# Filler matmuls on TensorE ahead of its waits in the gather passes of a four-layer graph network

## The chip, the cores and the metric

The kernel runs on one core of one Trainium2 chip. The metric is the device time of one execution in microseconds. Before the change it is 6958.88 us, the median of three runs (6939.15 to 6967.73).

## The reference

Four graph layers run one after the other over 6250 nodes of 128 features and 100,000 edges, sorted by their target. Each layer's result is added to its input and layer-normalised:

```python
edge_index = jnp.stack([src, dst])
x = _layernorm(x + L0(edge_index, x))              # attention of one head
x = _layernorm(x + L1(x, edge_index, edge_attr_3)) # attention of four heads
x = _layernorm(x + L2(x, edge_index))              # edge MLP
x = _layernorm(x + L3(x, edge_index, edge_weight)) # two graph convolutions
```

Every layer takes rows of a node table by an edge's index, weights them per edge, and sums them into the edge's other node (`segment_sum`): in L0 and L1 `h[src]` with softmax weights into `dst`, in L2 two SiLU products of both nodes' features into `row`, in L3 twice `h[row] * norm` into `col`.

## The kernel before

Between the gather passes stand short node passes, which do the dense products, the layer norm and write the table for the next pass to HBM. The gather passes take nearly all of the time. There are five of them, by four pieces of code: L0 (first pass, unrolled), L1 (second, a loop of four steps per turn), L2 (third, a loop of twelve groups per turn) and `convolution`, which is called twice.

In all of them GpSimd fetches edge tiles: one indirect DMA takes 128 rows of the table by 128 indices in `idx_now` into a ring in SBUF. L0 and L1 have 208 steps of four such gathers (`gather`, L664); L2 (L1852) and each convolution (L2246) have 784 gathers in groups of eight and 104 groups of steps. VectorE builds one-hot matrices of the target within a tile of 128 nodes (L934, L1998, L2313: tensor_scalar), TensorE multiplies them with the rows, which sums them by node (L1069, L1406, L1953, L2296), and VectorE adds the product from PSUM to `acc` (L965, L1436 and L1442, L2008, L2323). ScalarE weights the rows (`wide`) and copies the indices of later steps into `idx_now`, which lets GpSimd go on.

The order of each engine's work is the program's order; semaphores tie the engines to each other. On TensorE the steps are these:

- L0 `step`: wait for `l0_wide` (ScalarE) and `l0_acc` (VectorE), then four products (L1069), and in some steps eight transposes for a sort that VectorE runs beside the pass. `spread_last` multiplies once into banks 6 and 7, which VectorE reads as `pair[3]`.
- L1 `step`: the sum of the step two back (L1406), the queries of the next step (L1397), then wait for `l1_gm` and one product (L1417) that spreads the step's maximum; VectorE waits for it at L1489 in the same step.
- L2 `step`: `own_half` of the group two ahead (L1922, 24 products), `turn` of the next (L1932), `second_product` of this (L1937, L1941), `summed` of the one before (L1948, L1953).
- `convolution` `step`: wait for a cleared window, two zero products (L2290), wait for the one-hots and for the landed tiles (`rows_of` reads from a table how many are needed), eight sums (L2296), two closing products (L2299).

VectorE in L2 makes the transposed one-hots of a later group (L1981) as soon as TensorE has used up the older ones. After the sum of a convolution group it adds (L2323), clears the window (L2326) and makes the one-hots of the next group (L2313).

An fp32 product shows in the trace as two matmuls with a weight load each. PSUM has eight banks of 512 words per partition; `pair[n]` is banks 2n and 2n + 1.

## Time and profile before

| | us |
|---|---|
| median of the runs | 6958.88 |
| lowest and highest | 6939.15, 6967.73 |
| profiled execution, first to last instruction | 5685.5 |
| median less that span | 1273.4 |
| GpSimd busy | 3958.0 |
| VectorE busy | 3263.6 |
| TensorE busy | 3113.8 |
| ScalarE busy | 1491.5 |

The profile gives the span of its execution, and no time for the execution as a whole, so what the runs hold beside the span can only be had as a difference to their median. The page prints each engine's busy share in 40 slices and below them the clock that TensorE was granted (PEclk, in tenths of 2.4 GHz; 5 is 1.2 GHz). Matmuls overlap each other, so a mean duration times a count is more than the busy time. GpSimd's time in a gather is the making of the transfer, not the transfer.

### The profile page before, as it was taken

How to read it: one execution, taken by the hardware profiler on the slowest of the kernel's cores; microseconds unless marked ns; L12 is line 12 of the kernel's file. 1: busy time of each engine (PE TensorE's matmuls, PEld its weight loads, DVE VectorE, ACT ScalarE, POOL GpSimd, SP SyncE). 2: the span in 40 equal slices, each digit the busy share in tenths (PEclk: the TensorE clock that was granted, in tenths of full speed). 3: DMA queues.
4: the chain of work that ended last, by engine and by line, in shares of the span. 5: the costliest groups of instructions: out<-in, count | busy, mean ns of one | idle time of the engine just before them, and what ended most of it. 6: DMA issues, size and time to landing. Idle time of an engine off the chain costs nothing. (4 is left out here: it accounts for less than half of the span.)

```text
span 5685.5 us, 82572 instructions
## 1 busy us (share of the span) xinstructions
PE 3113.8 (55%) x17051; PEld 2734.5 (48%) x17052; DVE 3263.6 (57%) x12090; ACT 1491.5 (26%) x5626; POOL 3958.0 (70%) x4054
## 2 busy tenths in 40 slices
PE   4444444356666666778898988433333443333333
PEld 3333333345555555657777776333333343333332
DVE  6888887676787787744444444433444443344445
ACT  2333333345555555532222223100000000000001
POOL 3777777736777777367777772677777757777774
PEclk7555555568888777865555556666666666666666
DMA  5111112214444444222121110111111121111112
GB/s 123 52 52 52 52 52 56 49 52 131 132 132 131 130 131 131 70 54 56 52 56 51 53 52 21 56 52 51 51 51 51 51 61 52 51 51 51 51 51 57
DMA packets 222234, 385.68 MB, mean 68 GB/s; under 512 B 85452, under 2 KB 121882, under 8 KB 221998
## 3 DMA queue, kind: packets, MB, share of 16 engines
q0 software_dynamic: 142944, 296.35, 19.0%
q1 hardware_dynamic: 79054, 86.72, 5.0%
q8 instruction: 83, 1.36, 0.1%
q14 instruction: 153, 1.25, 0.1%
HBM read 356.23 MB, written 26.56 MB: 67 GB/s over the span
## 5 line engine op out<-in xcount | busy, mean ns | idle before, releaser
L2246 POOL DMA_INDIRECT arena<-table_gcn,idx_now x1568 | 1532.2, 977 | 642.9 <-issue 422.1
L2296 PE MATMUL pair<-arena,hotf 128*128 x3328 | 726.6, 408 | 1224.7 <-POOLq L1819 1199.3
L2296 PEld LDWEIGHTS pair<-arena,hotf 128*128 128x128 f32 x3328 | 691.2, 317 | 1256.1 <-issue 1255.8
L664 POOL DMA_INDIRECT arena<-table_attention,idx_now x832 | 825.7, 992 | 272.7 <-issue 197.2
L664 POOL DMA_INDIRECT arena<-table_key_value,idx_now x832 | 789.2, 949 | 275.9 <-issue 221.1
L1852 POOL DMA_INDIRECT arena<-table_edge_mlp,idx_now x784 | 768.1, 980 | 261.2 <-issue 212.4
L2323 DVE TENSOR_TENSOR acc<-acc,pair 128x1024 f32 x208 | 253.9, 1221 | 1133.9 <-PE pair L2299 1133.9
L1069 PE MATMUL pair<-wide,hotf 128*128 128x130 f32 x1664 | 431.0, 439 | 653.3 <-ACT wide L1033 653.3
L1069 PEld LDWEIGHTS pair<-wide,hotf 128*128 128x128 f32 x1664 | 369.0, 326 | 718.5 <-ACT wide L1033 718.5
L2256 ACT COPY idx_now<-src_t 128x8 int32 (+1 forms) x204 | 39.3, 197 | 1815.2 <-PE pair L2299 1803.2
L1406 PE MATMUL pair<-wide,hotf 128*128 128x132 f32 x1664 | 314.1, 347 | 232.9 <-DVE acc L1436 232.8
L1991 DVE TENSOR_TENSOR hot<-pair,arena 128x64 f32<-128x64 f32 x832 | 132.8, 224 | 492.1 <-POOLq L1819 456.7
L2313 DVE TENSOR_SCALAR hotf<-iota,rel_now,ew_now 128x128 f32<-128x128 f32 x1664 | 406.5, 331 | 0.0
L1406 PEld LDWEIGHTS pair<-wide,hotf 128*128 128x128 f32 x1664 | 267.6, 241 | 272.9 <-issue 270.5
L1953 PE MATMUL pair<-wide,hotf 128*128 128x64 f32 x1664 | 373.8, 418 | 0.0
L1953 PEld LDWEIGHTS pair<-wide,hotf 128*128 128x128 f32 x1664 | 354.6, 324 | 6.5
L1397 PE MATMUL pair<-arena 128*128 x1664 | 307.6, 347 | 8.5 <-DVE arena L1453 8.5
L1397 PEld LDWEIGHTS pair<-arena 128*128 128x128 f32 x1664 | 293.2, 264 | 9.1 <-issue 8.9
L1349 ACT ACTIVATE junk<-iota,rel_now 128x128 f32<-128x128 f32 x832 | 265.7, 390 | 18.3 <-ACT idx_now L652 12.9
L1033 ACT ACTIVATE wide<-arena,small 128x129 f32<-128x129 f32 x832 | 267.0, 393 | 0.0
L1468 DVE TENSOR_TENSOR junk<-pair,arena 128x512 f32<-128x512 f32 x208 | 143.9, 692 | 204.4 <-DMA arena<-table_key_value,idx_now 204.2
L938 DVE SCALAR_TENSOR_TENSOR junk<-iota,rel_now,arena 128x128 f32<-128x128 f32 x832 | 256.4, 344 | 0.0
(371 smaller groups left out, 5709.7 us busy)
## 6 DMA issues: line engine op xcount, KB each, us to landing
key<-rel_dram SPq DMA_DIRECT2D x104, 256.0 KB, 3.4
arena<-rel_dram SPq DMA_DIRECT2D x52, 512.0 KB, 3.7
arena<-table_gcn,idx_now POOLq DMA_INDIRECT x1568, 2.5
arena<-table_attention,idx_now POOLq DMA_INDIRECT x832
arena<-table_key_value,idx_now POOLq DMA_INDIRECT x832
arena<-table_edge_mlp,idx_now POOLq DMA_INDIRECT x784, 2.4
table_attention<-arena SPq DMA_DIRECT2D x13, 512.0 KB, 3.0
table_gcn<-acc SPq DMA_DIRECT2D x26, 256.0 KB, 2.3
```

What stands on the lines that cost most here:

```text
L664: q_.indirect_dma_start(ring[:, slot, 0:width], None, table, bass.IndirectOffsetOnAxis(ap=idx_now[:, slot:slot + 1].bitcast(U32), axis=0)) ...
L938: last = v.scalar_tensor_tensor(out=junk[:, 0, u * P:(u + 1) * P], in0=iota[:, :], scalar=rel_now[:, g * G + u:g * G + u + 1], in1=dst_sco ...
L1033: last = s_.activation(wide[:, g, u, 0:D + 1], ring[:, g * G + u, 0:D + 1], ACT.Identity, scale=small[:, g, u:u + 1])
L1069: last = t_.matmul(bank[2 * (g % 2) + u // 2][:, (u % 2) * AW:(u % 2) * AW + D + 2], hotf[:, g, u, :], wide[:, g, u, 0:D + 2], start=True, ...
L1349: last = s_.activation(away[:, u * P:(u + 1) * P], iota[:, :], ACT.Abs, scale=-1.0, bias=rel_now[:, g * G + u:g * G + u + 1])
L1397: last = t_.matmul(QB[g % 2][:, u * P:(u + 1) * P], hotT_f[:, g, u * P:(u + 1) * P], flat(look[:, bass.ds(nodes[u], 1), :]), start=True, s ...
L1406: last = t_.matmul(bank[SUM + 2 * (g % 2) + u // 2][:, (u % 2) * AW:(u % 2 + 1) * AW], hotf[:, g, u, :], wide[:, g, u, :], start=True, sto ...
L1852: q_.indirect_dma_start(mlp_ring[:, slot * EH:(slot + 1) * EH], None, t2, bass.IndirectOffsetOnAxis(ap=idx_now[:, slot:slot + 1].bitcast(U ...
L1953: last = t_.matmul(window[:, bass.ds(offset * EH, EH)], hot8[:, g % 2, u, :], s2[:, g % 2, u * EH:(u + 1) * EH], start=False, stop=(u == C ...
L2246: q_.indirect_dma_start(conv_ring[:, slot * D:(slot + 1) * D], None, table, bass.IndirectOffsetOnAxis(ap=idx_now[:, slot:slot + 1].bitcast ...
L2296: t_.matmul(window[:, bass.ds(offset * D, D)], hot8[:, g % 2, u, :], conv_ring[:, bass.ds(slot * D, D)], start=False, stop=False)
L2313: last = v.tensor_scalar(out=hot8[:, g % 2, u, :], in0=iota[:, :], scalar1=rel_now[:, at], scalar2=ew_now[:, at], op0=ALU.is_equal, op1=AL ...
```

## The change

A helper `keep_busy(spare, times)` issues matmuls of a constant bf16 identity with a constant bf16 row of numbers, repeated four times to 512 columns, into a PSUM bank. Nothing reads that bank's content. It is called on TensorE once per step in all gather passes: 12 times before the wait for `wide` in L0 (bank 7), 6 times before the wait for the maximum in L1 (bank 0), 10 times between `second_product` and `summed` in L2 (bank 3), and 24 times before the wait for the cleared window in the convolutions (bank 7). To leave bank 7 free in L0, `spread_last` goes to banks 4 and 5 and VectorE reads `pair[2]`. `rows_of` now loads its register and takes the maximum with 0 into a second one.

```diff
--- before.py
+++ after.py
@@ -688,6 +688,11 @@
                 batch(b, 2, 2)
             batch(NB - 2, 2, 1)
             batch(NB - 1, 2, 0)
+
+        def keep_busy(spare, times):
+
+            for _ in range(times):
+                t_.matmul(spare, ident_b[:, :], iota_b[:, :].unsqueeze(1).to_broadcast([P, 4, P]), start=True, stop=True)
 
         NORM = BT + 1
 
@@ -865,7 +870,7 @@
                     dve.wait_ge(sort_lastB, 1)
                     ch(v.scalar_tensor_tensor(out=key[:, :].rearrange("q (b p) -> q b p", **by_block),
                                               in0=iota[:, :].unsqueeze(1).to_broadcast([P, SORT // P, P]), scalar=float(SORT // P),
-                                              in1=pair[3][:, :].rearrange("q (b p) -> q b p", **by_block), op0=ALU.mult, op1=ALU.add))
+                                              in1=pair[2][:, :].rearrange("q (b p) -> q b p", **by_block), op0=ALU.mult, op1=ALU.add))
                     counts, e, node, base = (tiny[:, n, :] for n in range(4))
                     for b in range(SB):
                         yield
@@ -1058,11 +1063,12 @@
                     pe.wait_ge(pick_made, 1)
                     pe.wait_ge(sort_last, 1)
                     for h in range(2):
-                        last = t_.matmul(bank[6 + h], pick_last[:, :], last_tile[:, h * 512:(h + 1) * 512], start=True, stop=True)
+                        last = t_.matmul(bank[4 + h], pick_last[:, :], last_tile[:, h * 512:(h + 1) * 512], start=True, stop=True)
                     last.then_inc(sort_lastB, 1)
 
                 def step(i, g, past, left):
                     k = i * RING + g
+                    keep_busy(bank[7], 12)
                     pe.wait_ge(l0_wide, k + 1)
                     pe.wait_ge(l0_acc[G - 1], k + 1)
                     for u in range(G):
@@ -1413,6 +1419,7 @@
                         summed(*later(i, g, -2))
                     if left:
                         query(*later(i, g, 1))
+                    keep_busy(bank[0], 6)
                     pe.wait_ge(l1_gm, k + 1)
                     t_.matmul(MB[:, 0:P], small[:, g, 0:1].to_broadcast([P, P]), ident[:, :], start=True, stop=True).then_inc(l1_gmB, 1)
 
@@ -1822,8 +1829,10 @@
 
         def rows_of(eng, need, table, k):
 
-            eng.reg_load([need], table[0:1, bass.ds(k, 1)])
-            return eng.snap(need, min_val=0, max_val=CTILE_GROUPS - 1) + 1
+            loaded, bounded = need
+            eng.reg_load([loaded], table[0:1, bass.ds(k, 1)])
+            eng.reg_alu(bounded, loaded, 0, ALU.max)
+            return eng.snap(bounded, min_val=0, max_val=CTILE_GROUPS - 1) + 1
 
         def at_least(eng, signal, k, more):
 
@@ -1960,6 +1969,7 @@
                     if not isinstance(k, int) or k + 1 < CSTEP_GROUPS:
                         turn(k + 1, g + 1)
                     second_product(k, g)
+                    keep_busy(bank[3], 10)
                     if not isinstance(k, int) or k > 0:
                         summed(k - 1, g - 1 + CRING)
 
@@ -1973,7 +1983,7 @@
             def _(dve):
                 first = [dve.alloc_register(f"l2_node{g}") for g in range(2)]
                 slots = [dve.alloc_register(f"l2_slot{u}") for u in range(CG)]
-                need = dve.alloc_register("l2_need")
+                need = [dve.alloc_register(f"l2_need{n}") for n in range(2)]
 
                 def hot_look(i, g, k):
                     dve.wait_ge(l2_rel_in[g % 4 // 2], 16 * (k // 4 + 1) if isinstance(k, int) else 4 * k - 4 * (g % 4) + 16)
@@ -2279,12 +2289,13 @@
                 def _(pe):
                     slots = [pe.alloc_register(f"{name}_slot{u}") for u in range(CG)]
                     offsets = [pe.alloc_register(f"{name}_offset{u}") for u in range(CG)]
-                    need = pe.alloc_register(f"{name}_need")
+                    need = [pe.alloc_register(f"{name}_need{n}") for n in range(2)]
 
                     def step(i, g, k):
                         window = pair[g % 3]
                         pe.reg_load(slots, step_slot[0:1, bass.ds(k * CG, CG)])
                         pe.reg_load(offsets, step_offset[0:1, bass.ds(k * CG, CG)])
+                        keep_busy(bank[7], 24)
                         pe.wait_ge(cleared, k + 1)
                         for h in range(2):
                             t_.matmul(window[:, h * 512:h * 512 + D], zeros[:, 0:P], zeros[:, 0:D], start=True, stop=False)
```

## Rows read from the trace of the kernel before

**Rows 1.** The page, 40 slices: GpSimd's busy tenths, TensorE's granted clock in tenths.

```profile
POOL 3777777736777777367777772677777757777774
PEclk7555555568888777865555556666666666666666
```

**Rows 2.** Windows, four passes: stretch, PE, PEld, DVE, ACT, POOL busy, clock, DMA, GB/s.

```profile
102.60:1199.50 1096.90, 457.23 (x1785) 392.86 (x1786) 846.21 (x4115) 409.29 (x1884) 832.30 (x839) 0.51 0.21 52
1305.50:2347.80 1042.30, 677.45 (x3719) 608.14 (x3719) 822.74 (x2883) 559.43 (x2073) 789.17 (x832) 0.80 0.44 131
2450.90:3457.70 1006.80, 872.08 (x5516) 752.37 (x5517) 440.10 (x1936) 201.62 (x501) 768.11 (x784) 0.52 0.19 53
3583.80:4588.30 1004.50, 389.04 (x2060) 359.76 (x2060) 419.73 (x1050) 39.81 (x296) 765.88 (x784) 0.67 0.18 51
```

**Rows 3.** Timeline: start us, us, engine, line, operation, idle time before.

```profile
4016.84 0.94 POOL L2246 DMA_INDIRECT arena<-table_gcn,idx_now  x1 [0.30 <-issue]
...
3421.25 1.47 POOL L1852 DMA_INDIRECT arena<-table_edge_mlp,idx_now  x1 [0.30 <-DMA arena<-table_edge_mlp,idx_now]
3421.49 0.42 DVE L1981 TENSOR_SCALAR hotT<-arena,part 128x1024 bf16<-128x1024 bf16 x1
```

**Rows 4.** Grouped lines, GpSimd's gathers: busy us, mean ns | idle before.

```profile
L2246 POOL DMA_INDIRECT arena<-table_gcn,idx_now x1568 | 1532.2, 977 | 642.9 <-issue 422.1 <-ACT ew_now L2261 165.6 <-DMA arena<-table_gcn,idx_now 55.2
L664 POOL DMA_INDIRECT arena<-table_attention,idx_now x832 | 825.7, 992 | 272.7 <-issue 197.2 <-DMA arena<-table_attention,idx_now 42.7 <-ACT idx_now L652 32.8
L664 POOL DMA_INDIRECT arena<-table_key_value,idx_now x832 | 789.2, 949 | 275.9 <-issue 221.1 <-DMA arena<-table_key_value,idx_now 31.7 <-ACT idx_now L652 23.1
L1852 POOL DMA_INDIRECT arena<-table_edge_mlp,idx_now x784 | 768.1, 980 | 261.2 <-issue 212.4 <-DMA arena<-table_edge_mlp,idx_now 26.2 <-ACT rel_now L1878 22.6
```

**Rows 5.** Waits: engine, line, releaser: us in total, times, longest.

```profile
PE pair L2296 <- POOLq L1819: 1199.3, 192, 12.2
...
DVE junk L1468 <- DMA arena<-table_key_value,idx_now: 204.2, 206, 4.1
```

**Rows 6.** Timeline, third pass: 24 matmuls of 64 columns, one of 512, bf16.

```profile
2943.98 1.49 PE L1922 MATMUL pair<-arena,hotT 128*128 x24
...
2947.45 0.60 PE L1937 MATMUL pair<-tab 3*128 3x512 bf16 x1
```

**Rows 7.** Timeline, second pass: L1417 at 1.2 GHz, then a step at 2.4.

```profile
1705.20 0.80 PE L1417 MATMUL pair<-ident,small 128*128 128x128 f32 x2
...
1707.01 1.14 PE L1406 MATMUL pair<-wide,hotf 128*128 128x132 f32 x8 [1.01 <-DVE acc L1436]
...
1707.98 1.05 PE L1397 MATMUL pair<-arena 128*128 x8
...
1710.28 0.49 PE L1417 MATMUL pair<-ident,small 128*128 128x128 f32 x2 [1.24 <-DVE small L1480]
```

**Rows 8.** Timeline, convolutions: a group's matmuls at either clock.

```profile
4006.73 3.55 PE L2296 MATMUL pair<-arena,hotf 128*128 x16 [2.42 <-POOLq L1819]
...
5628.43 2.23 PE L2296 MATMUL pair<-arena,hotf 128*128 x16
...
5636.12 3.49 PEld L2296 LDWEIGHTS pair<-arena,hotf 128*128 128x128 f32 x16 [4.51 <-issue]
```

**Rows 9.** Windows of 1 us: a convolution group, then the third pass.

```profile
4006.00:4007.00 1.00, 0.27 (x1) 0.30 (x2) 1.00 (x3) 0.00 (x0) 0.70 (x2) 0.76 0.21 57
...
4010.00:4011.00 1.00, 0.55 (x7) 0.25 (x5) 0.44 (x1) 0.39 (x3) 0.70 (x2) 1.00 0.02 4
...
2943.00:2944.00 1.00, 1.00 (x7) 1.00 (x7) 0.00 (x0) 0.00 (x0) 0.94 (x1) 0.50 0.16 33
```

**Rows 10.** Timeline, ends of the third and the first pass.

```profile
3464.26 1.06 PE L1932 MATMUL pair<-ident,junk 128*128 128x128 f32 x4
...
3481.85 0.69 DVE L2008 TENSOR_TENSOR acc<-acc,pair 128x512 f32 x1 [3.08 <-PE pair L1953]
...
1204.18 2.10 PE L1069 MATMUL pair<-wide,hotf 128*128 128x130 f32 x8 [3.86 <-ACT wide L1033]
```

## Prediction

> **What bounds the kernel now.** I read the page first. GpSimd's busy tenths stand at 7 in nearly every slice except at the ends of stages; TensorE's granted clock changes from slice to slice while GpSimd's share does not [rows 1]. So I cut the span into its gather passes, one stretch each [rows 2]; of the two convolutions, which are alike, one stands. They hold 1096.9 + 1042.3 + 1006.8 + 2 x 1004.5 = 5155 us of the span of 5685.5, and in each GpSimd is busy for 76% although TensorE's busy time runs from 389 to 872 us and its clock from 0.51 to 0.80. The rest of GpSimd's time is a fixed gap: the timeline shows a gather of 0.94 us with 0.30 us of "issue" before it, over and over, 1.25 us a gather with rounding [rows 3]. The grouped lines give 832 + 832 + 784 + 1568 = 4016 gathers [rows 4]. 4016 x 1.25 = 5020 us, and the means above 0.94 us account for most of what is left: 832 x 0.05 + 832 x 0.01 + 784 x 0.04 + 1568 x 0.035 = 136 us. That is 5156, the length of the passes. The kernel is paced by GpSimd issuing gathers back to back, and the waits of TensorE (1199 us for landed groups in the convolutions) are those of a faster engine for that pace [rows 5]. The longest wait of VectorE in the second pass, 204 us for gathered rows in 206 steps, says the same: about 1.0 us of slack in each step of 5.0 us [rows 5].
>
> **What TensorE would have to do.** The change puts filler matmuls on TensorE, which is in order: the wait behind the filler, and everything behind that wait, comes after it. The executed filler is 208 x 12 = 2496 matmuls in the first pass, 208 x 6 = 1248 in the second, 104 x 10 = 1040 in the third and 208 x 24 = 4992 in the two convolutions. A filler matmul streams 512 bf16 columns over one weight load. The trace has no such stream. The nearest is 24 bf16 matmuls of 64 columns in 1.49 us at the low clock, 62 ns or 0.97 ns a column, so 512 columns cost some 0.43 us at 1.2 GHz (columns over clock) and 0.21 us at 2.4 GHz (an estimate from that row and the two clock levels). The upper end is a lone 512-column bf16 matmul at 0.60 us [rows 6]. Now the budget of one step:
> - First pass: period 5.0 us (4 gathers); own matmuls 2.10 us at 1.2 GHz [rows 10], so half of it at 2.4; filler 12 x 0.43 = 5.1 or 12 x 0.21 = 2.6. Sum 7.2 or 3.6 us.
> - Second pass: period 5.0; own 1.14 + 1.05 + 0.49 less overlap = 2.5 at the high clock [rows 7]. The pass's busy time is 677/1042 of 5.0 = 3.25 at a mean clock of 0.80, that is 60% high and 40% low, so 0.6 x 2.5 + 0.4 x 4.4, and 4.4 at the low clock. Filler 2.6 or 1.3. Sum 7.0 or 3.8.
> - Third pass: period 10.0 (8 gathers); own 872/1007 of 10.0 = 8.7 at a mean clock of 0.52, or about 4.5; filler 4.3 or 2.1. Sum 13.0 or 6.6 [rows 2].
> - Convolutions: period 10.0; own 3.55 + 0.3 = 3.8 (high clock 2.23 + 0.3 = 2.5); filler 10.2 or 5.1. Sum 14.0 or 7.6 [rows 8].
>
> So at 2.4 GHz all four fit under the gathers and at 1.2 GHz none does. The whole change hangs on the granted clock. A mean clock of 0.5 x 13.0/10 = 0.65 is enough in the third pass, and 0.70 to 0.72 by the same working in the others.
>
> **Will the clock rise?** In a convolution the clock fell in the microsecond from 4006 (0.76), after TensorE had waited 2.42 us. Then a burst of 128-column matmuls began at 4006.73 and took 3.55 us, and in the microsecond from 4010 the clock was 1.00 again [rows 8, 9]. In the second pass, where TensorE works 65% of the time, the mean is 0.80. Against this stands the third pass: TensorE busy for 1.00 of a microsecond again and again and the clock still 0.50 [rows 9]. Much of that pass's work (L1922, L1953) loads 128 columns of weights to stream 64, so the array itself is fed half of the time. The filler streams 512 columns per load and is denser than what raised the clock in the convolutions, 24 and 12 of them in a row. And the mechanism corrects itself: a TensorE that falls behind at 1.2 GHz has no idle time at all, only dense filler and its own work. I take the clock to be near 1.0 in the first pass and the convolutions, 0.9 in the second, 0.7 to 0.9 in the third, where only a third of the time is filler and TensorE has the largest own load. The Trainium skill, TensorE: Matmul & The Clock Gate, Part 1, says that activity releases the throttle and idleness brings it back; the third pass shows that busy time as the profile counts it is not yet that activity.
>
> **What a faster TensorE is worth.** In the passes nothing directly: every microsecond that it gains it waits longer for GpSimd. Three things remain.
>
> Drains, the work after the last gather of a pass. Third pass: the last gather ends at 3457.7, VectorE's last add starts at 3481.85, and TensorE is the chain: turn, product, sum, product, sum, sum. From the turn at 3464.26 that is 17.5 us; at 2.4 GHz 8.8 + 2 fillers x 2.1 = 13.0, so -5 us (at 1.2 GHz 17.5 + 2 x 4.3, so +9) [rows 10]. First pass: the last four products, 2.10 us, halve: -1. Second pass: two such groups on the path: -2. Convolutions: the last three sums start some 3.8 us apart, at 5628.43 and, after a wait for the last tiles, at 5636.12. With 2.2 + 5.1 us before each of the last two, the last starts near 5624.6 + 2 x 7.5 = 5639.6, 3.5 us later than now, and takes 1.3 us less: +2 each [rows 8, 10]. Sum -1 - 2 - 5 + 2 + 2 = -4.
>
> Stretched gathers. Some gathers take up to 1.47 us instead of 0.94, when a VectorE tensor_scalar starts inside the first part of a gather: L1981 at 3421.49 in that from 3421.25 [rows 3]. L2313 does the same in the convolutions. The same instructions starting in the gap or late in a gather cost nothing. By the means against a plain gather's 0.944 us the excess is 0.036 x 784 = 28 us in the third pass and 0.033 x 1568 = 52 us in the convolutions [rows 4]. The start of these instructions follows TensorE: in the third pass L1981 comes after TensorE's `own_half`, which now queues behind 8.7 us of work a group; in the convolutions L2313 follows the sum by the add and the memset. With a faster TensorE the third pass's L1981 comes straight after the memset, another phase, and I book half of the 28 us: -14. In the convolutions the sum shortens from 3.5 to 2.2 us, 1.3 us, nearly one gather period of 1.25, so the phase stays almost where it is; I book -4 of the 52, with -52 and +20 as bounds (none hit; each of 196 groups 0.1 us worse). In the first pass these starts follow the landing and not TensorE: 0. The Trainium skill, SBUF — State Buffer, "Who interferes with whom", has this as a lock: VectorE in a two-port mode and GpSimd exclude each other for a whole instruction. The trace agrees in kind (0.42 us of VectorE cost GpSimd 0.53 us). The same section gives TensorE read ports of its own, by which the filler would slow nothing directly; no row here shows that.
>
> Rest: the moved bank of `spread_last` (once), one register operation more per step in front of a wait, and a program longer by the filler. 0, because TensorE's and VectorE's queues wait for landed groups there.
>
> Sum: -4 - 14 - 4 = -22 us against the profiled span of 5685.5, so 5664. The profiled execution's own time is not given beside its span; the median of the runs is 6958.9, 1273.4 us more than the span, and no row says what lies there. I carry it unchanged: 6958.9 - 22 = 6937. The three runs spread over 29 us, so about 0.5%, 35 us, is what a measurement of this kernel can tell from no change.
>
> **Rivals.**
> 1. The collisions with VectorE vanish in the convolutions too. For it: only the start's phase counts, and any other phase than the first half of a gather is free. Against: the shift of 1.3 us lands on the same phase. Price -4 - 28 - 52 = -84: 6875 at full size, some -50 at half. With the forecast's own upper part this is what makes the change faster by over 35 us.
> 2. The filler makes the second pass slower. There the filler stands right ahead of the matmul L1417, whose result VectorE waits for in the same step. At 2.4 GHz TensorE now idles 1.24 us before that matmul and the filler needs 1.3: it just fits. At 1.2 GHz there is no idle time (the matmul at 1705.20 shows none before it), so the filler's 2.6 us come on top; VectorE has 1.0 us of slack, so 1.6 us are lost [rows 5, 7]. The pass has a mean of 0.80, so 40% of the time is at the low clock: 208 x 0.4 x 1.6 = 133 us, giving 7070. It decides if the low clock still stands in more than a tenth of the steps (21 x 1.6 = 33 us). Against it: with the filler TensorE is idle for 1.2 us of 5.0 at the high clock, where it now is for 2.5.
> 3. The change doesn't do what it says: the filler does not hold the clock up, above all in the third pass, where a busy TensorE stayed at 0.50. TensorE becomes the bound of that pass: 104 x (13.0 - 10.0) = 312 us at worst, half of it if the clock rises at times; 7115 to 7270.
>
> **Chances.** Forecast, gathers still pace all passes and the time moves by less than 35 us: 0.60. Rival 1, or other collision savings large enough: 0.25. Rival 2 in some size: 0.10. Rival 3: 0.05. Faster by over 0.5% 0.25, within 0.5% 0.60, slower 0.15. The range reaches from rival 1 at three quarters of its size, 6895, to a small share of rival 2, 6995; what it leaves out is the full rivals 2 and 3 and the deepest part of rival 1, about 0.2.
>
> **What would show it.** Right: gather starts still 1.25 us apart and the five passes within 20 us of their length; TensorE's clock above 0.85 in the first pass and the convolutions; TensorE's busy share at 70% or more everywhere with its waits for landed groups much shorter; the mean of L1852's gathers nearer 0.95 and that of L2246's still 0.97; the third pass's drain some 5 us shorter, the convolutions' 2 us longer. Wrong: GpSimd waiting for ScalarE's `idx_now` inside a pass; a wait of VectorE at L1489 for L1417 of more than 0.1 us a step; a granted clock under 0.65 in the third pass; or a part outside the span that moves, which this trace cannot price.

## The result, and the profile after

The changed kernel takes 7324.52 us (median of four runs, 7320.3 to 7351.38) against 6959.17 us before (four runs, 6939.15 to 6967.73): a ratio of 1.0533, 95% interval 1.0504 to 1.0562. The forecast was 6937 us, its range 6895 to 6995: wrong, and in the direction that had a chance of 0.15.

From the page, 40 slices of the changed kernel: busy tenths of TensorE and GpSimd, and the granted clock in tenths.

```profile
span 7318.6 us, 102124 instructions
...
PE   5677666776666656658888789767777786777777
...
POOL 3555555525555555445555553166666626666662
PEclk7788788788888888777777777878888887888888
```

The clock did rise, from the 5 to 8 of [rows 1] to 7 or 8. But GpSimd, 7 in nearly every slice before, is mostly at 4 to 6: it waits inside the passes. And this execution took 7320.48 us with a span of 7318.6: 1.9 us lie outside the span. In every run below it is 1.8 or 1.9. So the 1273 us that the forecast set "beside the span" of 5685.5 can't lie there; the execution traced before was of another speed than the timed ones. The windows of the five passes, from first to last gather, columns as in [rows 2]:

```profile
107.50:1525.70 1418.20, 961.26 (x4221) 514.81 (x4219) 843.56 (x4068) 403.73 (x1869) 817.24 (x839) 0.79 0.18 41
1639.00:3076.10 1437.10, 877.43 (x4936) 684.61 (x4936) 826.53 (x2867) 567.96 (x2067) 804.84 (x832) 0.84 0.33 95
3185.20:4507.40 1322.20, 1051.61 (x5992) 695.92 (x5993) 411.76 (x1782) 179.05 (x469) 754.75 (x784) 0.74 0.16 40
4712.10:5896.50 1184.40, 880.52 (x4105) 452.60 (x4104) 379.47 (x950) 37.06 (x276) 754.72 (x784) 0.82 0.17 44
6009.20:7194.00 1184.80, 883.32 (x4113) 451.12 (x4112) 371.45 (x938) 36.47 (x276) 752.71 (x784) 0.81 0.17 43
```

GpSimd's own busy time in them is that of [rows 2] (817 against 832, 755 against 768), yet each is 180 to 395 us longer. TensorE isn't full: 961 of 1418, 880 of 1184. What they wait for (engine, line, releaser: us, times, longest):

```profile
ACT idx_now L2266 <- remote: 1766.6, 109, 49.5
DVE acc L2334 <- remote: 1331.2, 109, 45.6
...
POOL arena L2256 <- ACT ew_now L2271: 726.5, 110, 204.6
POOL arena L664 <- ACT idx_now L652: 722.7, 149, 22.8
```

Behind GpSimd stands ScalarE's `idx_now`, behind that the end of TensorE's sum ("remote" is a releaser that the profile can't name). The timeline of one convolution group shows why the sum ends late (L2307 is L2296 of before, L695 is the filler, below):

```profile
5019.40 1.49 PE L2307 MATMUL pair<-arena,hotf 128*128 x11
...
5021.21 0.27 PE L2307 MATMUL pair<-arena,hotf 128*128 x1 [0.32 <-issue]
...
5021.92 0.37 PE L2307 MATMUL pair<-arena,hotf 128*128 x1 [0.44 <-issue]
...
5022.63 0.27 PE L2307 MATMUL pair<-arena,hotf 128*128 x1 [0.34 <-issue]
...
5025.45 0.27 PE L2307 MATMUL pair<-arena,hotf 128*128 x1 [1.74 <-issue]
...
5026.88 0.16 PE L2310 MATMUL pair<-wide 1*128 1x2 bf16 x1 [1.05 <-issue]
```

Eleven of the sixteen run in 1.49 us. Then single ones start 0.71 us apart (5021.21, 5021.92, 5022.63) and the closing product is done at 5027, 7.6 us after the first. Nothing holds them that the profile shows: the idle time before them is put down to "issue". I read that as TensorE waiting for its own instructions, which is an inference. The same kernel, run again (e5 below), took 5738.59 us, and there the sixteen products of a convolution group, and the 24 fillers behind them, take:

```profile
5019.97 2.27 PE L2307 MATMUL pair<-arena,hotf 128*128 x16 [1.32 <-POOLq L1826]
...
5023.30 5.34 PE L695 MATMUL pair<-iota_b,ident_b 128*128 128x512 bf16 x24 [0.93 <-issue]
```

**Two levels.** All kernels below come beside runs of the kernel before on the same chip, and those fall at two levels that no edit makes: 5667, 5669, 5692 and 5669 us in four sets of runs, 6962 and 7072 in two. One chip was at 5669 in one set and at 6962 in another, so the level isn't the chip's. I call them quick and late (for the late instructions that I infer). The recorded result stands at the late level, the trace of before at the quick one. The change costs at both, by different routes.

### The profile page after: what moved, and what is told of

Read it like the earlier page. It is cut to its first block and busy times, and to the rows that moved or that the text cites. A ratio compares the mean times of both kernels' runs of the same rounds, so it can differ in the third digit from the quotient of the medians.

```text
span 7318.6 us, 102124 instructions
## 1 busy us (share of the span) xinstructions
PE 5239.2 (72%) x26827; PEld 3211.4 (44%) x26828; DVE 3284.5 (45%) x12090; ACT 1490.9 (20%) x5626; POOL 3920.6 (54%) x4054
## 3 DMA queue, kind: packets, MB, share of 16 engines
q8 instruction: 153, 2.51, 0.1%
## 5 line engine op out<-in xcount | busy, mean ns | idle before, releaser
L695 PE MATMUL pair<-iota_b,ident_b 128*128 128x512 bf16 x9776 | 2760.5, 431 | 457.1 <-issue 434.0
L695 PEld LDWEIGHTS pair<-iota_b,ident_b 128*128 128x128 bf16 x9776 | 1031.9, 108 | 1907.4 <-issue 1182.3
L2307 PE MATMUL pair<-arena,hotf 128*128 x3328 | 515.2, 304 | 248.5 <-issue 242.8
L2307 PEld LDWEIGHTS pair<-arena,hotf 128*128 128x128 f32 x3328 | 453.6, 211 | 279.0 <-issue 260.7
L1075 PE MATMUL pair<-wide,hotf 128*128 128x130 f32 x1664 | 289.1, 319 | 320.6 <-ACT wide L1038 186.4
L1412 PEld LDWEIGHTS pair<-wide,hotf 128*128 128x128 f32 x1664 | 255.7, 232 | 583.4 <-issue 582.2
L970 DVE TENSOR_TENSOR acc<-acc,pair 128x130 f32 x832 | 238.6, 287 | 482.2 <-remote 408.1
L1931 PE MATMUL pair<-arena,hotT 128*128 x2496 | 301.6, 205 | 189.1 <-issue 179.3
L1075 PEld LDWEIGHTS pair<-wide,hotf 128*128 128x128 f32 x1664 | 253.2, 222 | 402.9 <-ACT wide L1038 241.5
L1931 PEld LDWEIGHTS pair<-arena,hotT 128*128 128x128 bf16 x2496 | 218.8, 100 | 265.4 <-issue 200.1
L1496 DVE TENSOR_REDUCE small<-pair 128x1 f32<-128x128 f32 x208 | 60.6, 291 | 564.3 <-remote 407.4
L2018 DVE TENSOR_TENSOR acc<-acc,pair 128x512 f32 x104 | 71.4, 686 | 527.0 <-DMA key<-rel_dram 317.8
```

The source lines that it names most:

```text
L695: t_.matmul(spare, ident_b[:, :], iota_b[:, :].unsqueeze(1).to_broadcast([P, 4, P]), start=True, stop=True)
L970: v.tensor_add(here, here, bank[2 * (g % 2) + u // 2][:, (u % 2) * AW:(u % 2) * AW + D + 2]).then_inc(l0_acc[u], 1)
L1075: last = t_.matmul(bank[2 * (g % 2) + u // 2][:, (u % 2) * AW:(u % 2) * AW + D + 2], hotf[:, g, u, :], wide[:, g, u, 0:D + 2], start=True, ...
L1412: last = t_.matmul(bank[SUM + 2 * (g % 2) + u // 2][:, (u % 2) * AW:(u % 2 + 1) * AW], hotf[:, g, u, :], wide[:, g, u, :], start=True, sto ...
L1931: last = t_.matmul(LB[g % 2][:, u * EH:(u + 1) * EH], hotT8[:, g % 2, u * P:(u + 1) * P], flat(look2[:, bass.ds(node, 1), c * EH:(c + 1) * ...
L2307: t_.matmul(window[:, bass.ds(offset * D, D)], hot8[:, g % 2, u, :], conv_ring[:, bass.ds(slot * D, D)], start=False, stop=False)
```

## Experiments at the quick level

**e1, the edits without a filler.**

```diff
-            for _ in range(times):
+            for _ in range(0):
```

> The change without a single filler matmul: the moved bank of spread_last and the extra register step of rows_of stay. Theory A (the filler matmuls themselves cost the time, by whatever path): ratio to before within 0.5% of 1. Theory B (the small edits cost it, the register step stands in front of TensorE's and VectorE's waits 312 times): a good part of the 5.3% stays, ratio 1.02 to 1.05. In the trace theory A wants no TensorE instructions spaced 0.70 to 0.71 us apart, as they are in the trace of the changed kernel in runs of five to ten.

5666.0 against 5667.14 us, ratio 1.0000 [0.9989, 1.0011]. The moved bank and the extra register operations cost nothing.

**e2, narrow filler everywhere; e3, a quarter of it (3, 2, 2, 6); e4, the convolutions' filler alone.**

```diff
-    t_.matmul(spare, ident_b[:, :], iota_b[:, :].unsqueeze(1).to_broadcast([P, 4, P]), ...)
+    t_.matmul(spare[:, 0:64], ident_b[:, :], iota_b[:, 0:64], ...)
```

for e2, for e3

```diff
-            for _ in range(times):
+            for _ in range(times // 4 if times > 6 else 2):
```

and in e4 the other three calls of `keep_busy` are left out.

> All 9776 filler matmuls, each of 64 columns instead of 512: the same number of instructions, an eighth of the array's work. Theory S (supply: TensorE's instruction stream, their number, is what stalls, in runs of instructions 0.71 us apart): about as slow as the change, ratio 1.03 to 1.06. Theory L (load: 512 columns at a clock that is 1.2 GHz for part of the time are too much work): ratio 0.99 to 1.01, with gathers 1.25 us apart and each pass as long as in the trace of before.

> A quarter of the filler: 3, 2, 2 and 6 matmuls of 512 columns instead of 12, 6, 10 and 24. Both the load and the number of instructions fall. Theory L: TensorE needs at most 2.10 + 1.3, 4.4 + 0.9, 8.7 + 0.9 and 3.8 + 2.6 us of a period of 5, 5, 10 and 10 us even at 1.2 GHz, so only the second pass could be held up, by little: ratio 1.00 to 1.01. Theory S, if the cost goes by the number of filler instructions: a quarter of 5.3%, ratio 1.013.

> Filler only in the two convolutions, 24 a group. In the changed kernel's trace a convolution takes about 1255 us where the trace of before has 1005. If the passes cost their part independently and the trace of before is what the timed runs do, 500 us come on top, ratio 1.07; if the loss of 365 us spreads over the passes by their filler, 4992 of 9776 matmuls, half of it, ratio 1.026. The three passes without filler should look as in the trace of before, 1097, 1042 and 1007 us; if they don't, something other than the filler stretches them.

e2: 1.0002 [0.9992, 1.0012]; e3: 0.9997 [0.9986, 1.0009]; e4: 5660.19 us, 0.9984 [0.9974, 0.9994], 7 us faster, where I had expected 1.026 or 1.07 from the late level's trace. So at this level neither the filler's instructions alone (e2) nor a quarter of the filler (e3) costs anything. GpSimd's grouped gathers of the convolutions, e1 and then e4:

```profile
L2256 POOL DMA_INDIRECT arena<-table_gcn,idx_now x1568 | 1535.6, 979 | 637.9 <-issue 427.0 <-ACT ew_now L2271 161.9 <-DMA arena<-table_gcn,idx_now 49.1
```

```profile
L2253 POOL DMA_INDIRECT arena<-table_gcn,idx_now x1568 | 1521.4, 970 | 645.7 <-issue 429.7 <-ACT ew_now L2268 168.7 <-DMA arena<-table_gcn,idx_now 47.2
```

The gathers are 14 us shorter together: 151 of them take more than 1.05 us, against 187 in e1, so fewer collide with VectorE. From the first gather to the last the two convolutions take 2037.4 us against 2052.5, and the wait at their seam is about the same (38.8 us against 39.7). The 7 us more under `ew_now` are the wait ahead of the first convolution, 129.6 us against 121.0, where no filler runs; without filler in the third pass it is anything from 117 to 130 us (before, e1 to e4, e6, e7). So the traces show a gain of about 15 us in the convolutions, of which 7 show in the medians; the two traced spans are 3 us apart.

**e5, the changed kernel again; e6, e7, e8, the filler in the first, the second, the third pass alone.** In e8, and likewise in e6 and e7:

```diff
-                    keep_busy(bank[7], 12)
...
-                    keep_busy(bank[0], 6)
...
-                        keep_busy(bank[7], 24)
```

> The changed kernel as it is, on a chip where the kernel before takes what its trace shows (5667 us, four runs of experiments so far) and not 6959. Theory C (the loss belongs to chips or times in which TensorE's instructions are held back, at 0.71 us each; without that the gathers pace all passes): ratio 0.990 to 1.005, spans near 5650, as my sum had it, and no runs of instructions 0.71 us apart. Theory F (the full filler does it anywhere, above all in the first three passes, since filler in the convolutions alone gave 0.998): ratio 1.05 or above.

> Filler only in the first pass, 12 a step. Theory F: the pass is 1418 us long in the changed kernel's trace against 1097, so some of that stays here, up to +320 us, ratio up to 1.056. Theory C: ratio 0.997 to 1.002, the pass 1090 to 1100 us, clock near 1.0.

> Filler only in the second pass, 6 a step, ahead of L1417. My second rival (the filler delays L1417 whenever the clock is low): +10 to +130 us, ratio 1.002 to 1.023, VectorE waiting at L1496 for L1424. Forecast: ratio 0.999 to 1.001 and the pass 1042 us long. Theory F: up to +395 us.

> Filler only in the third pass, 10 a group. My third rival (the clock stays at 0.50 and TensorE becomes the bound): +150 to +312 us, ratio 1.03 to 1.055. Forecast: clock 0.7 to 0.9, the drain 5 us shorter and stretched gathers rarer, -5 to -30 us, ratio 0.995 to 0.999.

e5: 5738.59 against 5669.12 us, 1.0128 [1.0111, 1.0145], between the 0.990 to 1.005 and the 1.05 that my two theories had. e6: 0.9996 [0.9986, 1.0006]. e7: 1.0006 [0.9996, 1.0016]. e8: 5748.47, 1.0145 [1.0128, 1.0162], where I had expected less than 1, or 1.03 and more. The third pass holds the whole loss. Yet its window in e5 is no longer than in [rows 2]:

```profile
103.10:1193.00 1089.90, 806.45 (x4271) 451.14 (x4270) 846.60 (x4115) 409.50 (x1884) 825.06 (x839) 0.97 0.23 53
1299.00:2340.20 1041.20, 776.70 (x4960) 557.86 (x4960) 822.28 (x2881) 557.18 (x2071) 788.06 (x832) 0.99 0.45 131
2443.10:3441.10 998.00, 960.34 (x5986) 664.67 (x5987) 413.06 (x1782) 179.72 (x469) 753.95 (x784) 0.82 0.21 53
3641.20:4641.00 999.80, 810.93 (x4511) 465.67 (x4509) 419.61 (x1049) 39.81 (x296) 761.18 (x784) 1.00 0.20 52
4680.00:5679.80 999.80, 815.94 (x4507) 468.14 (x4506) 411.86 (x1037) 39.23 (x296) 761.13 (x784) 0.99 0.20 52
```

TensorE is busy for 960 of the third pass's 998 us, at 0.82 of the clock. The gathers run ahead of it through the ring, so what it falls behind shows after the last of them, at 3441.1. VectorE's last add in e5:

```profile
3540.24 0.69 DVE L2018 TENSOR_TENSOR acc<-acc,pair 128x512 f32 x1 [1.37 <-PE pair L1962]
```

That is 99 us behind the last gather; in the trace of before it is 24 (3457.7 to 3481.85, [rows 10]), in e1, the same program without filler, 19. Against e1's trace the account closes: the third pass is 7 us longer (998.0 against 990.9), the way from its last gather to the first of the convolutions 79 us longer (200.1 against 121.0), the convolutions are 14 us shorter, and that makes the 72 us between the two spans (5732.7 and 5660.5). e8, which has no gain in the convolutions, lost 79 us by the medians. One group of that pass in e5, inside the pass:

```profile
2941.12 0.20 PE L1957 MATMUL pair<-wide 1*128 1x64 bf16 x1
2941.24 2.00 PE L1962 MATMUL pair<-wide,hotf 128*128 128x64 f32 x16
2943.08 2.53 PE L1931 MATMUL pair<-arena,hotT 128*128 x24
2945.57 0.86 PE L1941 MATMUL pair<-ident,junk 128*128 128x128 f32 x4
2946.36 0.60 PE L1946 MATMUL pair<-tab 3*128 3x512 bf16 x1
2946.89 2.08 PE L1950 MATMUL pair<-we,tab 128*128 128x128 f32 x8
2948.76 2.57 PE L695 MATMUL pair<-iota_b,ident_b 128*128 128x512 bf16 x10
2951.26 0.20 PE L1957 MATMUL pair<-wide 1*128 1x64 bf16 x1
```

2951.26 - 2941.12 = 10.14 us, without a gap. There are 98 groups of gathers for 104 of steps, 998 us of gathers in all, so 9.6 us a step is what keeps up; at 10.14 us a group, 104 groups leave a backlog of some 57 us, the greater part of the 79. The filler is as cheap as forecast. The odd term is `own_half`, L1931: 2.53 us, at a clock that the windows of 1 us (length, TensorE busy, clock, DMA, GB/s) give as full until it ends:

```profile
2944.00:2945.00 1.00, 1.00 (x9) 1.00 0.02 2
2945.00:2946.00 1.00, 1.00 (x8) 0.92 0.16 39
2946.00:2947.00 1.00, 1.00 (x4) 0.50 0.69 197
...
2948.00:2949.00 1.00, 1.00 (x6) 0.50 0.22 72
```

The same 24 took 1.49 us at the low clock [rows 6], and in e1, behind sixteen float32 products that the low clock stretched:

```profile
2943.77 3.68 PE L1962 MATMUL pair<-wide,hotf 128*128 128x64 f32 x16
2947.24 1.49 PE L1931 MATMUL pair<-arena,hotT 128*128 x24
```

Each of the 24 has the looked-up node as a register in its operand's address. Behind the stretch of e5 the clock is at 0.50 (1.2 GHz) for some 3 us, in which L1946 and L1950 run at their old durations. Why it falls is not shown. The traces have equally slow stretches that no fall follows: 2.35, 2.41 and 2.51 us in the groups of e5 from 3482 to 3502, and 2.60 and 2.69 us in k2 (five fillers a group, below) at 2940.86 and 2948.40.

**j2, the third pass's filler with a fixed node; j1, the changed kernel beside it.**

```diff
-                    pe.reg_load(nodes, step2_node[0:1, bass.ds(k * CG, CG)])
...
-                        node = pe.snap(nodes[u], min_val=0, max_val=NT - 1)
+                        node = 0
```

> The changed kernel once more, to have its ratio beside the level that the kernel before has in these runs. If before takes about 5667 us: 1.013, all of it in the third pass. If before takes 6950 us or more (TensorE's instructions arriving with gaps): 1.05. A filler that keeps all 9,776 instructions and an eighth of the columns gave 1.036 at a level of 7072 us, and one with 5,200 instruction records and all the columns gave 1.032: at that level this run says what share of its loss each of them kept.

> Only the third pass keeps its filler of 10, and the own-half multiplications all look up node 0 with no register in their addresses and no register loads (part of the computation is wrong). If before takes about 5667 us here, where the third pass with filler alone gave 1.0145: by the theory that the 24 own-half multiplications are held back by their issue with a register in the address, they take 1.5 us or less and not 2.5 a group, a group takes 9 us or less and not 10.15, and the ratio is 1.000 to 1.004; by the rival, that TensorE has too many columns and instructions in a group whatever the addresses, it stays 1.012 or more. If before takes 6950 us or more, the ratio is near 1.000, as it was (0.9988).

j1: 5740.52 against 5692.35, 1.0082 [1.0065, 1.0099]; before is slower in this set than beside e5, the change is not. j2, in which every `own_half` looks up node 0: 5688.75, 0.9995 [0.9985, 1.0004], with all ten fillers a group in place. In j2:

```profile
2957.51 2.00 PE L1959 MATMUL pair<-wide,hotf 128*128 128x64 f32 x16
2959.35 0.86 PE L1928 MATMUL pair<-arena,hotT 128*128 128x64 bf16 x24
2960.05 0.64 PE L1938 MATMUL pair<-ident,junk 128*128 128x128 f32 x4
```

0.86 us in place of 2.5, and TensorE's busy time between 2500 and 3400 us falls from 879 (j1) to 750. So the look-up by register (the eight loads and the register in each address, which j2 removes together) is what makes `own_half` long, by 1.7 us a group, and with it goes the loss. It isn't node 0 that makes them quick: in i2 below, 24 fillers of the same 64 columns, at a constant address, take 0.86 us as well (at 6019.51).

**k1, the same columns of filler in 5,200 matmul records for 9,776** (float32 products of 512 columns, each two records, in place of four bf16 ones); **k2, five fillers in the third pass alone.**

```diff
-            for _ in range(times):
+            for _ in range(times // 4):
+                t_.matmul(spare, ident[:, :], iota[:, :].unsqueeze(1).to_broadcast([P, 4, P]), ...)
+            for _ in range(times % 4):
```

> The changed kernel with all its columns of filler in 5,200 instruction records in place of 9,776 (four bf16 multiplications made one of float32). If before takes about 5670 to 5690 us here: the third pass's filler is 8 of 10 in float32, the own half still has a register in each address, so by the theory (the 24 own-half multiplications held back by their addresses, and TensorE full with them) most of the loss stays: own half 2.3 us or more, ratio 1.006 to 1.013; by the rival, that the number of filler instructions is what fills TensorE's sequencer, own half 1.6 us or less and ratio 0.998 to 1.003. If before takes about 6960 us here: comparable with the 1.0533 of the change at that level; the share of the loss that goes is the share that the number of instructions had.

> Only the third pass keeps its filler, 5 multiplications a group. If before takes about 5670 to 5690 us here: 10 made a group 10.15 us of TensorE against some 9.6 us a step of gathers; 5 fewer make it about 8.9 us, TensorE idles again at the turn (L1941), and the ratio is 0.999 to 1.002; if the loss were a fixed one for having the filler in that pass at all, it is 1.005 or more. If before takes about 6960 us here: 1.000, as it was (1.0005).

k1: 1.0136 [1.0116, 1.0156], no better than e5, with `own_half` at 2.6 us and a group at 10.3: the number of filler instructions isn't what fills the third pass. k2: 0.9991 [0.9981, 1.0000]. In k2 `own_half` is still slow, but this group is 7.5 us (2940.86 to 2948.40):

```profile
2940.86 2.60 PE L1929 MATMUL pair<-arena,hotT 128*128 x24
...
2945.26 1.24 PE L695 MATMUL pair<-iota_b,ident_b 128*128 128x512 bf16 x5
...
2948.40 2.69 PE L1929 MATMUL pair<-arena,hotT 128*128 x24
```

So a slow `own_half` alone costs nothing. It is the sum of it, the stretch at the low clock and ten fillers that passes 9.6 us.

## Experiments at the late level

h1 is k2's kernel, h2 is j2's; i1 is k1's, i2 is e2's.

**h1, h2, h3 (thirty fillers of 64 columns in the third pass alone), h4 (the change without the third pass's filler).** h3 has e2's narrow multiplication and no other filler than

```diff
-                    keep_busy(bank[3], 10)
+                    keep_busy(bank[3], 30)
```

and h4 only leaves that call out.

> Only the third pass keeps its filler, 5 multiplications of 512 columns a group and not 10. With 10 a group took 10.15 us of TensorE against some 9.6 us that GpSimd's gathers leave a step. If TensorE's own time decides (my theory), 5 fewer take off some 1.3 us or more: 8.9 us a group, below 9.6, so the pass ends as in the kernel before and the time is within 0.2% of it (ratio 0.999 to 1.002). If instead the filler costs by being there at all (the bank, the weights of the one-hot taking the place of the others, the clock), about half of the loss remains: ratio 1.006 to 1.008.

> Only the third pass keeps its filler, all 10; the pass's own-half multiplications no longer read which node they look up (eight register loads a group and a register in each operand's address left out): all look up node 0, so part of the computation is wrong. Theory: the 24 multiplications of a group take 2.3 to 2.7 us with the filler, although the clock is high at first, because TensorE's sequencer cannot issue those with a register in the address fast enough, and the clock falls behind this thin stretch. Then they take 1.5 us or less here, the clock falls for less of a group, and most of the loss goes: ratio 1.000 to 1.005. Rival: the register is not it, but the number of instructions (each multiplication and its weights) or the filler's own columns; then they stay at 2.3 us or more and the ratio stays 1.012 to 1.016.

> Only the third pass keeps a filler, of 30 multiplications of 64 columns a group in place of 10 of 512: 1,920 columns and not 5,120, but 20 more instructions. If columns are what a group has too many of, this costs nothing (ratio 0.999 to 1.002), as 10 of 64 columns in all passes did. If what limits TensorE is how fast its multiplications and weight loads are issued (the 24 of the own half took about 100 ns each with the filler), 30 of them take some 3 us, a group takes 10.5 us or more, and the loss is as large as with 10 wide ones or larger: ratio 1.015 to 1.03.

> The filler is left out of the third pass alone and stands in the first (12), the second (6) and the convolutions (24). The whole loss was seen in the third pass, where the filler makes TensorE the bound; the convolutions alone with filler were 0.9984 of the time before, first and second alone 1.000. So I expect 0.998 (0.997 to 1.000), which would be the best version. If the loss instead comes from the sum of the filler in all passes (heat, or a clock that is lowered for it later), it stays above 1.005.

Beside 6961.68 us: h1 1.0005 [0.9986, 1.0024]; h2 0.9988 [0.9965, 1.0011]; h3 1.0104 [1.0075, 1.0132]; h4 7263.5 us, 1.0453 [1.0428, 1.0479]. The fourth is a plain miss: I expected the best version. h3's thirty narrow fillers a group cost more than h1's five wide ones, but less than the 1.015 expected: its third pass and the wait behind it are 53 us longer than h1's. Another 36 us lie in its first two passes, where neither has filler, so that much two executions can differ here. h1 has almost no filler and stands for the kernel before at this level. Its first three passes and both convolutions:

```profile
106.40:1443.50 1337.10, 453.28 (x1771) 389.98 (x1771) 856.14 (x4083) 406.32 (x1875) 817.57 (x839) 0.51 0.19 43
1552.20:2929.00 1376.80, 720.67 (x3700) 663.00 (x3700) 825.80 (x2867) 559.32 (x2067) 811.10 (x832) 0.70 0.35 99
3033.50:4312.80 1279.30, 961.35 (x5519) 678.20 (x5519) 410.56 (x1782) 177.91 (x465) 760.18 (x784) 0.66 0.18 42
4501.30:6861.40 2360.10, 913.50 (x4129) 725.14 (x4130) 811.16 (x2027) 82.56 (x602) 1528.28 (x1568) 0.57 0.18 45
```

In k2, the same program at the quick level, the span is 5655.8 us and the passes take 1087, 1043, 991 and 2051. The busy times of VectorE, ScalarE and GpSimd agree within 1% in the two traces; TensorE's is 3452 us against 3121, at a lower clock. A convolution group of h1, in which TensorE has no filler:

```profile
5999.97 1.19 PE L2304 MATMUL pair<-arena,hotf 128*128 x4 [2.47 <-issue]
...
6001.57 1.19 PE L2304 MATMUL pair<-arena,hotf 128*128 x4 [0.41 <-issue]
...
6005.05 0.77 PE L2304 MATMUL pair<-arena,hotf 128*128 x2 [0.69 <-issue]
...
6007.08 0.21 PE L2307 MATMUL pair<-wide 1*128 1x2 bf16 x2
```

So in a kernel with almost no filler, too, TensorE's products start late at this level with nothing named that holds them, and the 1.0 us of slack a step is used up: GpSimd waited for ScalarE's `idx_now` (L652) for 609.8 us in h1, 55.6 in k2. Here more instructions ahead of a sum have a price. The changed kernel against h1, in us:

| stretch | change | h1 | more |
|---|---|---|---|
| first pass | 1418.2 | 1337.1 | 81 |
| second pass | 1437.1 | 1376.8 | 60 |
| third pass | 1322.2 | 1279.3 | 43 |
| last gather there to next gather | 204.7 | 188.5 | 16 |
| both convolutions | 2481.9 | 2360.1 | 122 |
| last gather to the end | 124.6 | 86.9 | 38 |
| the rest | 329.9 | 319.6 | 10 |
| span | 7318.6 | 6948.3 | 370 |

Of the 122 us of both convolutions, 81 lie in their two passes (1184.5 and 1184.8 us against 1144.2 and 1143.6) and 41 at the seam between them (112.7 against 72.2). Per step or group that makes 0.39 us for 12 fillers, 0.29 for 6, 0.39 for 24 (81/208), and 0.41 for 10 against 5. The seam and the end (38 us) are of another kind. TensorE is eleven groups behind the last gather there, and in the changed kernel it works them off without a gap, each with its 24 fillers (5.35 us), at 7.6 us a group:

```profile
5904.89 0.20 PE L2310 MATMUL pair<-wide 1*128 1x2 bf16 x2
...
5912.50 0.20 PE L2310 MATMUL pair<-wide 1*128 1x2 bf16 x2
```

In e5, at the quick level, only two groups are left behind that gather, so there the ends cost nothing. h4's third pass is 1267.4 us, and its span 75.6 us below the change's: about the third pass's own share here.

**i1 and i2**, a quarter of the instructions at the same columns, and the same instructions with an eighth of the columns.

> The changed kernel with the same columns of filler in about a quarter of the instructions: four multiplications of 512 bf16 columns are made one of 512 float32 columns (3 in place of 12, 1 and 2 narrow ones in place of 6, 2 and 2 in place of 10, 6 in place of 24). Theory for a chip where the time before is near 6960 us: there TensorE's instructions reach it with gaps of about 0.71 us, and every group pays for the instructions that the filler adds. Then the loss of the first, the second and the convolution passes (0.045 of the 0.053) mostly goes: ratio 0.995 to 1.015. Rival: the filler's busy time is what delays the groups there; then the ratio stays 1.04 or more. For a chip where the time before is near 5667 us: the third pass has its instructions spaced less closely; by the theory that issue bounds it the 24 own-half multiplications go back to 1.5 us and the ratio is 1.000 to 1.006, by the rival (columns saturate TensorE) it stays 1.012 or more.

> The changed kernel with all 9,776 filler multiplications, each of 64 columns and not 512: the same instructions, an eighth of the columns. On a chip where the time before is near 5667 us it gave 1.0002. Where it is near 6960 us: by the theory that instructions are what costs there, nearly the whole loss stays (ratio 1.03 to 1.055); by the rival (TensorE's busy time) it goes (ratio 0.998 to 1.01).

i1: 7293.22 against 7071.78, 1.0322 [1.0282, 1.0362]. i2: 7350.73, 1.0364 [1.0318, 1.0410]. i2 is the clear one: the same program cost nothing at the quick level (e2, 1.0002), and its 24 fillers take 0.86 us at the full clock against 5.35. So instructions alone make a loss at the late level. The convolutions show both parts: i2's two passes there are as long as the change's (1185.1 and 1183.6 us), so in them the columns add nothing that shows, though the two sets differ in level (7072 us before, against 6959). But its seam and end (72.7 and 86.7 us) are h1's, because a group behind the last gather takes 4.1 us and not 7.6. So the 79 us of the change's 370 at those two places go by columns. i1 is inconclusive for the rest. It kept 5,200 records, half and not a quarter, since a float32 product is two; and neither the change nor a kernel without filler has a trace at 7072 us. How the rest of the 0.053 divides between instructions and columns stays open.

## Why the prediction was wrong

- **The level of the time: wrong, and the step that failed.** The prediction says: "The median of the runs is 6958.9, 1273.4 us more than the span ... I carry it unchanged." They lie inside the span, and most of them in the passes: h1 and k2, one program, differ by 1292 us of span, 250, 334, 288 and 309 of it in the first three passes and the convolutions. So the 1273 us are time in which GpSimd does not gather back to back, the waits of TensorE are no longer those of a faster engine, and every budget was made against steps of 5.0 and 10.0 us that the timed kernel did not have (6.4, 6.6, 12.3 and 11.0 us in h1). There the filler cost 81, 60, 43 and 81 us in the passes and 95 behind them, the change against h1. The words "a part outside the span that moves, which this trace cannot price" named the hole and put it in the wrong place.
- **The clock: right at the quick level, too high for the timed one.** In e5 it is 0.97, 0.99, 0.82, 1.00 and 0.99; I had near 1.0, 0.9, 0.7 to 0.9, near 1.0. In the changed kernel's own trace it is 0.79, 0.84, 0.74, 0.82 and 0.81. That the array is "fed half of the time" in the third pass doesn't follow from [rows 6]: 64 columns at 1.2 GHz are 53 of the 62 ns of such a matmul.
- **The filler's price: right.** 5.34 us for 24 is 0.22 each, against 0.21. The budgets of the first and second pass and of the convolutions hold at the quick level: e6 and e7 are within 0.0006 of 1.
- **The third pass's budget: the term that failed at the quick level.** I halved TensorE's own 8.7 us to 4.5 for the high clock, had 6.6 with the filler, and set that against a period of 10.0, where 104 groups in 1006.8 us leave 9.7. A group of e5 at the full clock is 8.42 us (3488.78 to 3497.20), so its own part is 6.1, because `own_half` did not get shorter (2.41 us there); inside the pass the clock falls besides, and a group is 10.1. "-5 us" for that drain was +79.
- **Stretched gathers: mis-sized.** -14 us in the third pass: the mean of e5's gathers there is 962 ns, e1's 960, so nothing. -4 in the convolutions: -14 (e4).
- **The other drains:** +4 for the two convolutions, against nothing at the quick level: 39.0 us at the seam and 52.9 at the end in e5, 39.7 and 52.5 in e1. -1 and -2 for the first two passes, against nothing (106.0 and 102.8 us from last gather to next gather in e5, 106.0 and 103.0 in e1).
- **Rival 1** (collisions vanish): a quarter of its size for the convolutions, real but worth 0.16%. **Rival 2** (the filler ahead of L1417): absent at the quick level (e7). At the late level the second pass does lose, 60 us, though VectorE's wait at that place is no longer than without a filler (407.4 us in the change, 436.8 in h1); the mechanism was another, and isn't shown. **Rival 3** (TensorE becomes the bound of the third pass) came true at the quick level at a quarter of its price, though the clock did not stay at 0.5; at the late level the third pass and the wait behind it lose 59 us against h1.

The filler's price, and the clock at the quick level, were thus right and of no use for the result: a trace whose span is 1273 us short of the timed median is of another kind of execution than the one to be forecast.

**What stays open.** Why TensorE's instructions come late at one level. The amount of instructions fetched is no cause that shows: the instruction queue q8 moved 1.97 MB in h1 and in k2, 2.51 MB in the change and in e5. How long a fetch took at either level isn't shown, so slow fetches stay a rival that no run tested. That the filler's price there isn't simply so much an instruction (0.39 us for 12 and for 24) isn't explained either. Open, too, is what lowers the clock in the third pass while TensorE is busy throughout.

No version beats the kernel before at both levels: filler in the convolutions alone gains 0.16% at the quick one, and h4, which has it, loses 4.5% at the late one.

## What to carry to other kernels

First compare the traced execution's own time with the timed median. If they differ by more than the runs do, the slack read from the trace isn't the slack of the timed kernel, and an edit that spends slack must be priced for the worse of the two. Filler on an in-order engine is paid in issue as well as in columns: count the engine's time a group from rows at the high clock, and don't halve the stretches whose operands are addressed by a register (1.49 us at the low clock, 2.5 at the high one here). Where a ring lets the producer run ahead, look for an overfull consumer behind the last gather, not in the pass's length.

## What the runs showed of the hardware

- One kernel has two levels, each lasting over a set of runs, 5667 to 5692 and 6959 to 7072 us, some 23% apart. The same program at both (k2 and h1) has the same busy times of VectorE, ScalarE and GpSimd within 1%; at the slower level TensorE's matmuls in places start singly, in the changed kernel 0.71 us apart, with no wait that the profile names.
- 24 bf16 matmuls of 64 columns took 2.3 to 2.8 us (e5) with a register in the operand's address, at the full clock, and 0.86 us with a constant one (j2; i2's filler): about 100 ns against 36 each. Without filler, behind work at the low clock, the same 24 took 1.49 us. That TensorE's sequencer had run further ahead there is an inference.
- TensorE's clock fell to 1.2 GHz in the third pass (e5, from 2945 to 2949) although the engine was busy for 1.00 of each microsecond. In the group shown it fell behind the 24 thin matmuls of 64 columns; other such stretches kept the full clock. The Trainium skill, TensorE: Matmul & The Clock Gate, Part 1, ties the clock to activity; busy time as the profile counts it is again not that activity.
